# GpSimd's preparation of the attention results: one block before the softmax loop, or one step in each of its first nine slots

## The reference, cut to what matters

```
h = layernorm(x) * (1 + ca) + sa
x = x + ga * favor_attention(h)              # linear attention with random features
h = layernorm(x) * (1 + cb) + sb
for expert e in 0..3 (512 tokens each):      # second attention, softmax over all 2048 tokens
    m = 256 >> e
    q, k, v of these tokens from the first m features of layernorm(h)
attn = softmax(q @ k.T * scale) @ v          # 8 heads of 32
out_e = pad(attn[:, :m] @ o_w[:m, :m].T + o_b[:m]) + h
x = x + gb * out
```

## Time and profile before

| | |
|---|---|
| time, 3 runs | 2083.92 us median (2080.22 to 2085.06) |
| the profiled execution's own time | 2079.84 us |
| its span, first to last instruction | 2077.7 us |
| busy share of TensorE, VectorE, ScalarE, GpSimd | 87%, 73%, 52%, 48% |
| mean granted TensorE clock | 0.943 of full speed |

### The profile page before, as it was taken

The page is one execution under the profiler, slowest core; times in us unless marked ns, Lnnn a source line. Parts: engine busy times, 40 slices in busy tenths (PEclk is TensorE's granted clock), DMA queues, the critical chain, the costliest instruction groups (busy, mean ns, idle before and its releaser), DMA issues.

```text
span 2077.7 us, 29744 instructions
## 1 busy us (share of the span) xinstructions
PE 1807.0 (87%) x10752; PEld 1038.0 (50%) x10752; DVE 1512.4 (73%) x2733; ACT 1084.5 (52%) x1998; POOL 996.5 (48%) x654
## 2 busy tenths in 40 slices
PE   5788778999899886999989888699998887789997
PEld 3566443444377543444457744344436664434443
DVE  4688677777578677777668858777767876777774
ACT  0576233666567522566647743256665772326664
POOL 0333345666633245566753323666673332456666
PEclk8899888999999997999999999799999998889999
DMA  3000034001100015201020002500111000340011
GB/s 121 1 1 2 1 138 113 16 9 39 53 30 1 1 39 162 52 16 46 1 81 1 2 1 83 165 12 16 39 36 47 1 1 1 127 124 16 9 39 41
DMA packets 55705, 87.44 MB, mean 42 GB/s; under 512 B 13188, under 2 KB 32004, under 8 KB 52868
## 3 DMA queue, kind: packets, MB, share of 16 engines
q1 hardware_dynamic: 55560, 85.54, 14.1%
HBM read 49.68 MB, written 35.70 MB: 41 GB/s over the span
## 4 chain that ended last, share of the span: by engine, by line
PE 62%; DVE 21%; ACT 8%; issue 5%; DMA 2%; SPq 2%; POOL 1%; POOLq 0%; ACTq 0%; DVEq 0%
PE PS L1124 11%; PE PS L1249 11%; PE PS L1237 9%; PE PS L1262 5%; PE PS L1058 5%; PE PS L1026 5%; DVE MXP L812 4%; DVE XSQ L771 3%; PE PS L1050 3%; ACT XSQ L566 3%; PE PS L1167 3%; PE PS L1030 3%; DVE QKT L751 2%; PE PS L1194 2%; DVE QKS L862 2%
## 5 line engine op out<-in xcount | busy, mean ns | idle before, releaser
L812 DVE TENSOR_REDUCE MXP<-PS 128x1 f32<-128x512 f32 x960 | 598.4, 681 | 201.7 <-PE PS L1124 198.1
L471 POOL TENSOR_TENSOR TS<-PR 128x1024 f32<-128x1024 f32 (+1 forms) x256 | 573.5, 2240 | 335.8 <-ACT PR L637 335.8
L637 ACT ACTIVATE PR<-PS 128x512 f32<-128x512 f32 x960 | 504.8, 601 | 425.5 <-PE PS L1237 422.1
L1124 PE MATMUL PS<-KOP,QOP 96*128 96x512 f32 x960 | 422.6, 460 | 44.9 <-DMA KOP<-k_scr 34.3
L1237 PE MATMUL PS<-QOP,KOP 97*128 97x512 f32 x960 | 379.1, 408 | 17.9 <-ACT PR L637 12.7
L1124 PEld LDWEIGHTS PS<-KOP,QOP 96*128 96x128 f32 x960 | 190.6, 200 | 299.5 <-DVE MXP L812 176.6
L1249 PE MATMUL PS<-PR,V 128*32 128x512 f32 x1920 | 272.8, 605 | 0.0
L1058 PE MATMUL PS<-PB,QKT 128*128 128x512 f32 x768 | 221.8, 425 | 22.0 <-DVE QKT L751 22.0
L1237 PEld LDWEIGHTS PS<-QOP,KOP 97*128 97x128 f32 x960 | 181.0, 192 | 85.3 <-ACT PR L637 50.2
L428 POOL TENSOR_SCALAR PK<-XSK 128x1024 f32<-128x1024 f32 x64 | 67.7, 1058 | 283.4 <-ACT XSK L552 283.4
L1058 PEld LDWEIGHTS PS<-PB,QKT 128*128 128x128 f32 x768 | 140.8, 190 | 65.6 <-DVE QKT L751 38.8
(11 more groups left out here) (143 smaller groups left out, 2576.7 us busy)
## 6 DMA issues: line engine op xcount, KB each, us to landing
KOP<-k_scr SPq DMA_DIRECT2D x84, 256.0 KB, 6.1
k_scr<-QKS SPq DMA_DIRECT2D x64, 256.0 KB, 2.8
QOP<-q_scr SPq DMA_DIRECT2D x180, 64.0 KB, 2.0
q_scr<-QKS SPq DMA_DIRECT2D x40, 256.0 KB, 2.8
X<-in_L_attn_x_dram SPq DMA_DIRECT2D x16, 512.0 KB, 4.7
out_dram<-X SPq DMA_DIRECT2D x16, 512.0 KB, 3.2
QOP<-MXT SPq DMA_DIRECT2D x240, 0.5 KB
KOP<-k_scr SPq DMA_DIRECT2D x48, 64.0 KB, 2.0
```

The costliest lines, as they stand in the source:

```text
L471: g.tensor_tensor(sums(k)[:, 0:len(stage)], pair[:, :, 0], pair[:, :, 1], ALU.add).then_inc(S["psum_t"], 1)
L637: a.activation(PR[:, k % 2, w, q], bank(score_bank(p, n, w, q)), ACT.Exp).then_inc(S["ex"], 1)
L812: v.tensor_reduce(MXP[:, u % 2, i, kc:kc + 1], bank(max_bank(p)), AX.X, ALU.max).then_inc(S["am_rd"], 1)
L1124: mm(bank(max_bank(p)), QOP[0:96, u % QS6, i * P:(i + 1) * P], KOP[0:96, h % KS6, kc * CH:(kc + 1) * CH], start=True, stop=True).then_inc( ...
```

## The change

GpSimd now waits for the last low part of q and k (`q_lo`, 13 per batch element) where it waited for the last `x2`. Then it computes `OWG` and the base of the first result (expert 3) in one go. The other three bases, nine instructions, are done one by one, each behind the sum of one of slots 0 to 8. VectorE's wait for all bases moves from before slot 0 to the start of slot 9.

```
-                wait_all(pool, (S["x2"], NT * (b + 1)))
                 own_g = Chain(pool, S["pool_own"])
                 own_g.enter(b, PER_P)
                 gate = MODB[:, bass.ds(b, 1), 3, :]
+
+                def output_base(e, step):
+                    s, m = slot_of[e], width[e]
+                    if step == 0:
+                        own_g(g.tensor_tensor(Hh[:, slot(s), 0:m], Hh[:, slot(s), 0:m], OB[:, 0:m]
+                                              .rearrange("p (o d) -> p o d", o=1).broadcast_to([P, TPC, m]), ALU.add))
+                    elif step == 1:
+                        own_g(g.tensor_tensor(Hh[:, slot(s)], Hh[:, slot(s)], gate.broadcast_to([P, TPC, D]), ALU.mult))
+                    else:
+                        g.tensor_tensor(X[:, slot(s)], X[:, slot(s)], Hh[:, slot(s)], ALU.add).then_inc(S["base"], 1)
+
+                wait_all(pool, (S["q_lo"], NQ * (b + 1)))
                 own_g(g.tensor_tensor(OWG[:], OWT[:], gate.broadcast_to([P, KD, D]), ALU.mult))
-                for e in results:
-                    s, m = slot_of[e], width[e]
-                    own_g(... add OB)
-                    own_g(... times gate)
-                    g.tensor_tensor(X[:, slot(s)], X[:, slot(s)], Hh[:, slot(s)], ALU.add).then_inc(S["base"], 1)
-                own_g.leave(B)
+                for step in range(3):
+                    output_base(results[0], step)
 
                 for k in range(SLOTS):
...
                     g.tensor_tensor(sums(k)[:, 0:len(stage)], pair[:, :, 0], pair[:, :, 1], ALU.add
                                     ).then_inc(S["psum_t"], 1)
+                    if k < 3 * (NC - 1):
+                        output_base(results[1 + k // 3], k % 3)
+                        if k == 3 * (NC - 1) - 1:
+                            own_g.leave(B)
...
                 maxima((NC - 1) * EARLY, LOOK)
-                dve.wait_ge(S["base"], NC * (b + 1))
                 for k in range(SLOTS):
+                    if k == STEPS + 1:
+                        dve.wait_ge(S["base"], NC * (b + 1))
```

More of the change, by code:

```diff
@@ L455, in batch @@
                 gate = MODB[:, bass.ds(b, 1), 3, :]
-                own_g(g.tensor_tensor(OWG[:], OWT[:], gate.broadcast_to([P, KD, D]), ALU.mult))
-                for e in results:
-                    s, m = slot_of[e], width[e]
-                    own_g(g.tensor_tensor(Hh[:, slot(s), 0:m], Hh[:, slot(s), 0:m], OB[:, 0:m]
-                                          .rearrange("p (o d) -> p o d", o=1).broadcast_to([P, TPC, m]), ALU.add))
-                    own_g(g.tensor_tensor(Hh[:, slot(s)], Hh[:, slot(s)], gate.broadcast_to([P, TPC, D]), ALU.mult))
-                    g.tensor_tensor(X[:, slot(s)], X[:, slot(s)], Hh[:, slot(s)], ALU.add).then_inc(S["base"], 1)
-                own_g.leave(B)
+                def output_base(e, step):
[8 more added lines that the diff above has]
+                wait_all(pool, (S["q_lo"], NQ * (b + 1)))
+                own_g(g.tensor_tensor(OWG[:], OWT[:], gate.broadcast_to([P, KD, D]), ALU.mult))
+                for step in range(3):
+                    output_base(results[0], step)
                 for k in range(SLOTS):
```

## The result

The changed kernel takes 2102.47 us (median of 6 runs, 2100.29 to 2104.38), the kernel before 2081.93 us (6 runs, 2078.7 to 2085.06). The ratio is 1.0098, 95% interval 1.0085 to 1.0112: slower by 20.5 us. The profiled execution of the changed kernel took 2103.0 us, its span 2101.2 us, 23.5 us more than before.

The account below looks back on a forecast made before the run. TensorE bounds the loop, a serial chain of waits the stretch before it. 2079.84 - 9.2 + 20.0 + 5 = 2095.6 us for the profiled execution; the same +15.8 us on the median 2083.92 gives 2100 us, range 2087 to 2110.

Parts of the forecast that it names:

- The wait in slot 9: VectorE at slot 9's first maximum waits for the fourth base, and TensorE for VectorE: loss 20.0 us, ends 10 to 20.
- 29.4 us of GpSimd work: GpSimd's sums and spread base steps from slot 1 to slot 8, putting the fourth base at 362.4 in the first batch element.
- The first rival: Slot 9's wait is hidden by TensorE's other work or a GpSimd finished by 357.6: 2074.7 us, chance 0.08.
- The clock behind the wait: After TensorE's idle time in slot 9, slots 9 to 11 run at 1.2 GHz for 3 us: loss 5 us, ends 0 to 12.
- The gain in front: Ahead of slot 0, short low parts let block 12's store and slot 0 come earlier: gain 9.2 us, ends 0 to 16.8.
- 8.4 of the 9.2 us: Earlier issue of block 12's store in the four batch elements: 1.85 + 2.19 + 2.16 + 2.24 us; block 9 gives the other 0.8.
- the rest of the chain: Block 12's store, loads of KOP, four maxima and shift load up to slot 0: all serial, so saved time arrives at slot 0.
- Issue: SyncE gets to block 12's store at 311.03 instead of 312.88 in the first batch element, a gain of 1.85 us.
- The third rival: The low parts ahead of slot 0 shorten, but stores or loads behind them are late for another reason: 2109 us, chance 0.06.
- The contention: GpSimd's bases lengthen the last three low parts on VectorE to 6.27 us instead of 2.08, an excess of 4.2 us per batch element.
- the full wait that the prediction cites: The skill's rule that, of contending VectorE and GpSimd operations, the second one in fully waits for the first; by it 16.8 us return.

Follow-up runs that it names:

- wait_for_two: Changed kernel with spread bases in order of experts 0, 2, 1 and VectorE waiting in slot 9 for two bases, in slot 12 for all: 2081.88 us, ratio 1.0009.
- two_in_front: Changed kernel with the bases of experts 3 and 0 before the loop and the other two spread over slots 0 to 5: 2077.89 us, ratio 0.9995.
- low_from_psum: Kernel before with the low parts of blocks 10 to 12 computed from PSUM instead of TMP, without bias and scale: 2079.75 us, ratio 0.9997.
- loads_later: two_in_front with SyncE loading query units 2 to 5 behind the first shifts instead of in the middle stage: 2065.3 us, ratio 0.9927.
- loads_later_alone: Kernel before with only SyncE's edit of loads_later, GpSimd's block and VectorE's wait ahead of slot 0 as before: 2074.85 us, ratio 0.9975.
- busy_tensor: Changed kernel with 16 extra, unread matrix products on TensorE in slot 9 while it waits for VectorE: 2098.62 us, ratio 1.0093.
- spread_only: Changed kernel with GpSimd waiting for the last x2 again, spread steps and slot 9's wait kept: 2100.52 us, ratio 1.0103.

## Why the prediction was right, and where it was off

The forecast was 2100 us in 2087 to 2110, slower with a chance of 0.85; measured 2102.5. By the differences it is less close, 15.8 us forecast and 20.5 measured: the three runs that the forecast started from have a median of 2083.92, and the six of the result 2081.93. In the profiled executions the difference is 23.5 us, and its parts say more than the sum.

**The wait in slot 9** was the step that decided, and it held: 29.4 us of GpSimd work counted from slot 1's sum gave a fourth base at 362.4; in the changed kernel it ends at 361.58, where slot 1's sum starts 0.6 us earlier (332.36). That makes 29.2 us. The first rival, that it is hidden, is excluded by TensorE's 3.91 us of idle time.

That the stretch to slot 9 grew by 20.4 us against 20.0 is partly luck, since two things add up to it. The wait itself is the smaller 17.4 us: VectorE's idle time ahead of slot 9's first maximum grew from 1.44 us in each batch element to 5.74, 5.90, 5.74 and 5.74. The forecast of 20.0 counted from a slot 1 that starts as late as before. The other 3 us belong to the clock at the beginning of the loop, a term that the prediction didn't have. How long it stays low behind the first score differs from one batch element to the next, with steps of GpSimd in the slots and without. Here are the same 3 us in the kernel before, where slot 0 starts at 328.08, and in wait_for_two, where it starts at 328.97:

```profile
334.00:337.00 3.00, 3.00 (x14) 1.43 (x14) 2.60 (x7) 1.08 (x2) 0.97 (x2) 1.00 1.03 221
```

```profile
334.00:337.00 3.00, 3.00 (x8) 1.15 (x8) 1.66 (x5) 0.00 (x0) 2.92 (x3) 0.50 1.05 229
```

I took the low stretch behind the first score from the trace's clock record in the 24 batch elements of the six kernels whose sums and bases come in time (before, wait_for_two, two_in_front, low_from_psum, loads_later, loads_later_alone). The time from slot 0 to slot 9 is within 0.1 us of 27.3 us plus 0.41 us for each microsecond at the low level: 28.89 us with 3.96 low, 30.79 with 8.37. Summed over four batch elements the low stretch is 20.1 us in the profile before and 26.8 after, which is worth some 2.7 of the 20.4 us.

wait_for_two showed that it is this wait: with the same nine steps that stretch is 119.4 us, 2.1 more than before, of which the low clock (24.4 us instead of 20.1) explains 1.8. The steps themselves cost next to nothing.

**The clock behind the wait** was a term mis-sized: 5 us, measured 8.1. Per batch element I had 1.2 us; three of them lost 1.4 to 1.5 us and the third 3.8. I had reckoned with a low stretch of 3 us, as long as the window of the earlier trace rows; TensorE had the low level for 5.0 to 5.4 us after its return in three batch elements and for 10.2 us in the third (last section). busy_tensor ties the 8 us to the clock. The Trainium skill (TensorE: Matmul & The Clock Gate, What's actually happening) puts the ramp penalty at less than 1% of a typical kernel's span and says not to fit a model to a particular count of slow products. It says so of the ramp at a kernel's start; the 8.1 us here, behind an idle time in the middle of the loop, are 0.4% of the span of 2101 us and so within that figure, and yet a third of the 23.5 us.

**The gain in front** was the other mis-sized term: 9.2 us, measured 5.7 in this pair of profiles, and less than that where the change can act. Over the eight kernels of this study with short low parts and SyncE's old order (the changed one, and spread_only to low_from_psum) the time up to slot 0 is 1158.2 to 1162.9, mean 1161.0, which is 2.9 us less than before. Between the start of block 10's low part and slot 0, the only place where 8.4 of the 9.2 us could arise, the changed kernel has 84.2 us, 3.3 less than the kernel before, and the eight kernels on average 85.4, 2.1 less. What failed is the step that took the rest of the chain, from the issue of block 12's store to slot 0, to be as long as before ("everything on it is serial, so a microsecond saved in the low parts arrives at slot 0"). Issue was forecast well: 311.19 against 311.03. What I left out is what lies behind it. The four stores ahead now leave without gaps, and block 12's store comes into DMA engines that are full. The same 2 us before and after the change (columns of the earlier trace rows; the last two are the DMA engines' busy share and GB/s):

```profile
312.00:314.00 2.00, 0.00 (x0) 0.00 (x0) 2.00 (x4) 0.00 (x0) 1.92 (x2) 0.77 0.87 318
```

```profile
312.00:314.00 2.00, 0.00 (x0) 0.00 (x0) 1.52 (x3) 0.00 (x0) 2.00 (x1) 0.79 1.03 374
```

The store's first DMA is issued more slowly (0.74 against 0.32 us) and its second lands more slowly (3.37 against 2.74 us): 1.05 us of a gain of 1.7 in the first batch element. The slow issue goes with the unbroken row of stores: it takes 0.57 to 0.85 us in all 32 batch elements of the eight kernels, and 0.32 us in all 12 of the kernel before, loads_later and loads_later_alone, where SyncE pauses ahead of it. The engines' fill alone doesn't do it, since in loads_later they are just as full while the store is under way (1.06 in 310 to 312 us). The landing is open: 3.2 to 3.9 us in the eight kernels, 2.7 to 2.9 us in the kernel before and loads_later_alone, and 3.0 to 3.6 us in loads_later, so no run here separates the fill from the order of the DMAs. The third rival, late stores or loads behind short low parts, was thus partly true, and low_from_psum shows it without the change: low parts of 0.69 us and no time gained that could be told from nothing.

**The contention** itself was right. The Trainium skill (SBUF — State Buffer, Who interferes with whom) says that a tensor_tensor with both inputs in SBUF contends with GpSimd's reads while one with a single input there doesn't; low_from_psum agrees, 0.69 us against 1.67 to 2.86. The trace before also fits the full wait that the prediction cites: the three low parts end at 308.40, 311.19 and 312.85, each 0.54 to 0.56 us behind the end of a GpSimd instruction (307.86, 310.63 and 312.30).

## What to carry to other kernels

A wait for "all of it" on shared memory is paid by the last piece: before spreading work over a loop, add up the pieces up to the slot in which the wait stands, and order them so that the piece whose memory is needed first comes first. When a stall ends a chain of issues and transfers, follow the saved time through the queue to its last landing before it is counted; here low parts that were 16.8 us shorter brought some 2 us until the queue behind them was emptied, and the queue alone was worth a third of both together. An idle time of four microseconds on TensorE is to be priced with the low clock that follows it, here 8.1 us on 17.4 us of waiting: a third of the wait in three batch elements, nearly all of it again in one. And before a difference of two or three microseconds is given to an edit, look whether the clock came up at the same place in both profiles.

## What was not expected of the hardware

GpSimd's `OWG = OWT * gate` took 2.24 us before and takes 1.27 us in the changed kernel, where no low part runs beside it. Before, it started at 296.77 within a low part (296.60 to 297.29) that another one followed until 297.89; so the engine that came second was at times GpSimd. After:

```profile
310.01 1.27 POOL L467 TENSOR_TENSOR OWG<-OWT,MODB 128x512 f32<-128x512 f32 x1 [14.37 <-DVE QKS L872]
```

The low clock came back with TensorE in all four batch elements of the changed kernel, after 3.9 to 4.1 us of idle time in slot 9, and not equally long. In the first it was over by 368 us (above), in the third it lasted until 1388.3, 10.2 us after TensorE's return against 5.0 to 5.4 in the others. spread_only has two such batch elements, and 10.1 us in place of 8.1 behind the wait; what decides on the longer one, no run here shows. In the changed kernel the third batch element also has the longest stretch from slot 9 to the last score, 198.71 us against 196.35 to 196.47 in the others (columns of the earlier trace rows):

```profile
1378.00:1384.00 6.00, 5.84 (x17) 2.95 (x18) 5.13 (x11) 1.79 (x3) 2.36 (x1) 0.51 0.00 0
1384.00:1388.00 4.00, 4.00 (x19) 0.84 (x17) 1.10 (x2) 1.19 (x2) 2.33 (x1) 0.50 0.00 0
```
